# A decoder layer on one core: first keys turned by channel halves, and the opening of group 0 put in another order

## What is computed

```
x = layernorm(x + mixer(x))          # RMS norm, in-projection, causal conv of 4 taps, SiLU,
                                     # y = (C B^T * exp(cs_i - cs_j) * causal) (dt * hid) + D * hid,
                                     # gate, group RMS norm, out-projection
x = layernorm(x + softmax(x K^T) K)  # K: 1500 keys of 512 channels for each sequence
x = layernorm(x + ffn(x))            # base product + top-2 of 8 low-rank experts
```

## Time and profile before

| | |
|---|---|
| median of 3 runs | 1479.44 us (1477.43 to 1480.03) |
| the profiled execution's own time | 1479.15 us |
| its span | 1477.4 us |
| PE busy | 1420.3 us, 96% of the span |
| DVE, ACT, POOL busy | 67%, 51%, 34% |
| granted TensorE clock, mean | 0.99 |
| DMA | 142.60 MB, mean 97 GB/s |

### The profile page before, as it was taken

One profiled execution on the slowest core, in us unless ns is written; L12 is line 12 of the kernel. 1 busy time (PEld: TensorE's weight loads), 2 busy tenths in 40 slices (PEclk: granted clock), 3 DMA queues, 4 the chain that ended last, 5 costly groups with the idle time before them and its releaser, 6 DMA issues.

```text
span 1477.4 us, 30164 instructions
## 1 busy us (share of the span) xinstructions
PE 1420.3 (96%) x12816; PEld 1169.2 (79%) x12816; DVE 993.2 (67%) x1313; ACT 752.2 (51%) x1003; POOL 496.0 (34%) x368
## 2 busy tenths in 40 slices
PE   5899999999999999999999999999999978999995
PEld 4798989898989888888888888889888864445442
DVE  5784768476847684767476757765775676888764
ACT  5765636463756274636463656365536443543340
POOL 5253435242524253425342434333433320111101
PEclk9999999999999999999999999999999999999998
DMA  4431213121312131213221312221221365566610
GB/s 150 118 106 54 82 51 99 47 90 47 98 58 88 40 98 58 81 45 100 65 74 53 97 55 73 58 91 55 73 65 55 131 240 195 217 242 261 195 44 13
DMA packets 53347, 142.60 MB, mean 97 GB/s; under 512 B 9777, under 2 KB 9905, under 8 KB 46951
## 3 DMA queue, kind: packets, MB, share of 16 engines
q1 hardware_dynamic: 51518, 137.01, 28.3%
q0 software_dynamic: 1696, 3.67, 0.8%
HBM read 136.53 MB, written 2.29 MB: 94 GB/s over the span
## 4 chain that ended last, share of the span: by engine, by line
PE 83%; DVE 7%; issue 4%; DMA 3%; ACT 1%; POOL 1%; SPq 0%; DVEq 0%; POOLq 0%; ACTq 0%
PE bank L1174 47%; PE bank L1242 20%; PE bank L1217 5%; PE bank L1204 4%; DVE keysT L934 3%; DMA x1p<-acc 2%; PE bank L1477 2%; PE bank L1392 2%; PE bank L1448 1%; DMA ring_a<-in_context 1%; PE bank L1274 1%; DVE conv L809 1%; PE bank L1229 1%; PE bank L1444 0%; DVE part L770 0%
## 5 line engine op out<-in xcount | busy, mean ns | idle before, releaser
L1174 PE MATMUL bank<-h_hi,w_hi 128*128 128x448 f32 x1152 | 338.2, 375 | 2.2 <-DVE conv L809 2.2
L432 POOL TENSOR_TENSOR y_lo<-yg,y_hi 128x896 fp32r<-128x896 f32 x63 | 134.2, 2129 | 578.6 <-ACT y_hi L605 538.5
L1174 PE MATMUL bank<-h_lo,w_hi 128*128 128x448 f32 x1152 | 328.0, 366 | 0.0
L1174 PE MATMUL bank<-h_hi,w_lo 128*128 128x448 f32 x1152 | 327.1, 365 | 0.0
L809 DVE SCALAR_TENSOR_TENSOR conv<-bank,conv_w,conv 128x880 f32<-128x880 f32 (+2 forms) x240 | 268.0, 1117 | 85.6 <-ACT conv L578 79.8
L1174 PEld LDWEIGHTS bank<-h_hi,w_lo 128*128 128x128 f32 x1152 | 216.8, 188 | 17.4
L1174 PEld LDWEIGHTS bank<-h_lo,w_hi 128*128 128x128 f32 x1152 | 216.9, 188 | 17.2
L416 POOL TENSOR_TENSOR w_lo<-w_raw,w_hi 128x512 fp32r<-128x512 f32 x144 | 188.3, 1308 | 119.1 <-ACT w_hi L544 117.6
L1174 PEld LDWEIGHTS bank<-h_hi,w_hi 128*128 128x128 f32 x1152 | 208.2, 188 | 20.1 <-DVE conv L809 2.6
L854 DVE TENSOR_TENSOR hd_dt<-bank,dt_j 128x512 f32<-128x512 f32 x128 | 82.4, 685 | 208.0 <-PE bank L1204 208.0
L1242 PE MATMUL bank<-wo_hi,y_hi 128*128 128x512 f32 x420 | 165.2, 393 | 0.0
(11 more groups left out here) (181 smaller groups left out, 1932.1 us busy)
## 6 DMA issues: line engine op xcount, KB each, us to landing
w_raw<-in_w_in SPq DMA_DIRECT2D x144, 256.0 KB, 2.8
decay<-cs_scratch SPq DMA_DIRECT2D x128, 196.0 KB
ring_a<-in_context SPq DMA_DIRECT2D x24, 1024.0 KB, 7.9
ring_b<-in_context SPq DMA_DIRECT2D x21, 1024.0 KB
wo_raw<-in_w_out SPq DMA_DIRECT2D x64, 256.0 KB, 2.6
ring_b<-in_context SPq DMA_DIRECT2D x3, 896.0 KB
acc<-in_x SPq DMA_DIRECT2D x1, 1792.0 KB, 8.5
out<-z POOLq DMA_DIRECT2D x16, 112.0 KB, 2.7
```

The source lines that it names most:

```text
L432: g_.tensor_tensor(y_lo[:, c % 4, :], yg[:, c % 2, :], y_hi[:, c % 4, :].bitcast(f32), ALU.subtract).then_inc(s["y_low"], 1)
L1174: last = mm(place, w[:, k * P:(k + 1) * P], x[:, k, half * HALF:(half + 1) * HALF], start=(k == 0 and i == 0), stop=(k == KT - 1 and i == 2))
```

## The change

It touches two places, the opening with group 0, and the handover.

- `x` comes in three pieces (2, 2 and 3 tiles). The transposes of `x`, and the splits behind them, run over all channel blocks of tiles 0 to 3 first, then over all of tiles 4 to 6. POOL waits with its first split of a weight until all tiles are scaled. Several memsets and the two small operations at L940 and L941 stand first in DVE's queue.
- The conv taps of B and C stand ahead of the running sum on DVE. The copy to `cs_all` goes from DVE to ACT. The token-major transposes go behind `cb_product` (three of four) and `project(0, 4)` (the fourth), into four other banks. `mask_cb` of group 0 goes ahead of the differences, and the first five differences, distances and exponentials are spread over steps 0 to 2. The loads of weights 6 and 7 go ahead of the store of `cs_all`.
- At the handover, `keys_part(0, 0, 0)` goes ahead of the last two `add_skip`, and the order of the parts becomes: half 0 of unit 0, half 1 of unit 0, half 0 of units 1 and 2, half 1 of units 1 and 2. `score_first` makes each channel block over all keys at once, in the order 0, 4, 1, 5, 2, 6, 3, 7, then 8 to 15. `turn_first_queries` goes ahead of the last part of the out-projection. All remaining `last_sum`, and the statistics of tiles 1 to 3, are made before the loop over pairs, and the tiles' norms run one earlier all through the loop.

```diff
-            sp.dma_start(part[:, 0:4, :], x[:, 0:4, :]).then_inc(x_loaded[0], 16)
-            sp.dma_start(part[:, 4:TT, :], x[:, 4:TT, :]).then_inc(x_loaded[1], 16)
+            for i, (lo, hi) in enumerate(((0, 2), (2, 4), (4, TT))):
+                sp.dma_start(part[:, lo:hi, :], x[:, lo:hi, :]).then_inc(x_loaded[i], 16)
...
-            for idx in range(2, 6):
+            for idx in range(2, 8):
                 load_w(0, idx)
 
-            sp.wait_ge(s["dt_dve"], 6)
+            sp.wait_ge(s["cs_all_set"], 1)
...
+            pool.wait_ge(s["h_scaled"], TT)
             pool.wait_ge(s["dtw_hi"], 1)
...
             ln1_scale(1)
+            load_x1(1)
             ln1_scale(2)
-            load_x1(1)
+            ln1_scale(3)
...
                         first_tap(g, 2 + 2 * st, g * CT + st, 2 + st)
                         if first and st == 0:
-                            dt_token_major()
+                            act.wait_ge(s["dt_dve"], 5)
+                            a(real(cs_all), seqs(sq[:]), ACT.Copy).then_inc(s["cs_all_set"], 1)
+                        if first and st == 1:
+                            dt_token_major(3)
+                            exps(0, 0, 1)
...
                         if first and st == 0:
-                            for c in range(3):
-                                distance(0, c)
+                            for i in range(3):
+                                dt_token_major(i)
+                            distance(0, 0)
+                        if first and st == 1:
+                            distance(0, 1)
+                            distance(0, 2)
+                            exps(0, 1, 3)
+                        if first and st == 2:
+                            distance(0, 3)
+                            distance(0, 4)
+                            exps(0, 3, 4)
...
-            dve.wait_ge(s["dt_dve"], 4)
-            v.tensor_tensor_scan(sq[:], keep, yg[:, 0, :], 0.0, ALU.mult, ALU.add).then_inc(s["dt_dve"], 1)
-            dve.wait_ge(s["dt_dve"], 5)
-            v.tensor_copy(real(cs_all), seqs(sq[:])).then_inc(s["dt_dve"], 1)
+
+            def running_sum():
+                dve.wait_ge(s["dt_dve"], 4)
+                v.tensor_tensor_scan(sq[:], keep, yg[:, 0, :], 0.0, ALU.mult, ALU.add).then_inc(s["dt_dve"], 1)
...
                         taps(g, 1, g + GROUPS * CT + GROUPS, 1)
+                        if first:
+                            running_sum()
                     scale_hid(g, st - 1)
                     taps(g, 2 + 2 * st, g * CT + st, 2 + st)
                     wo_low(g, st - 2)
                     if first and st == 0:
-                        dve.wait_ge(s["cst_evac"], 4)
-                        for c in range(3):
-                            differences(0, c)
-                    differences(g, st + 3)
+                        mask_cb(0)
+                        dve.wait_ge(s["cst_evac"], 2)
+                        differences(0, 0)
+                    elif first and st == 1:
+                        weigh(0, 0)
+                        differences(0, 1)
+                        differences(0, 2)
...
+            keys_part(0, 0, 0)
             add_skip(LAST, CT - 2)
...
             wo_low(LAST, CT - 2)
-            keys_part(0, 0, 0)
+            keys_part(0, 0, 1)
...
-            keys_part(0, 0, 1)
+            keys_part(0, 1, 0)
             group_squares(GROUPS)
...
-            for half in range(2):
-                keys_part(0, 1, half)
+            keys_part(0, 2, 0)
+            keys_part(0, 1, 1)
+            keys_part(0, 2, 1)
             for t in range(4, TT):
                 last_halves(t)
-            for half in range(2):
-                keys_part(0, 2, half)
-            for t in range(1, 3):
+            for t in range(1, TT):
                 last_sum(t)
-                norm1_stats(t)
+                if t < 4:
+                    norm1_stats(t)
...
-                if u == 0:
-                    for t in range(3, TT):
-                        last_sum(t)
...
+            turn_first_queries()
             last_part(6, 7).then_inc(s["outb_done"], 1)
-            turn_first_queries()
...
-                for c in range(4):
-                    if c < 3:
-                        pe.wait_ge(s["q0_part"], c + 1)
-                    else:
+                for b in (0, 4, 1, 5, 2, 6, 3, 7):
+                    if b < 3:
+                        pe.wait_ge(s["q0_part"], b + 1)
+                    elif b == 3:
                         pe.wait_ge(s["q_set"], 1)
-                    if c == 0:
+                    if b == 0:
                         pe.wait_ge(s["kT_set"], 8)
-                    for k in range(KT):
-                        score_block(4 * k + c, 0, 2 * KB)
+                    last = score_block(b)
+                last.then_inc(s["s_mm"], 1)
                 pe.wait_ge(s["kT_set"], 12)
-                for b in range(NB):
-                    last = score_block(b, 2 * KB, KJ)
-                    if b % 8 == 7:
-                        last.then_inc(s["s_mm"], 1)
+                for b in range(8, NB):
+                    last = score_block(b)
+                last.then_inc(s["s_mm"], 1)
```

More of the change, by code:

```diff
@@ L530, in _ @@
             for t in range(TT):
[L531 removed]
+                act.wait_ge(x_loaded[min(t // 2, 2)], 16)
                 if t:
@@ L643, in group @@
                 for st in range(steps):
-                    if not (first and st == 0):
+                    if not (first and st < 3):
                         distance(g, st + 2)
-                    exp_step = live and st % 4 == 1
+                    exp_step = live and st % 4 == 1 and not (first and st == 1)
                     if exp_step:
@@ L740, in _ @@
             queries(0, range(4))
-            first_norm(1)
-            first_norm(2)
+            for t in range(1, 4):
+                first_norm(t)
             for u in range(PAIRS):
@@ L763, in _ @@
             v = nc.vector
+            v.memset(hid[:].rearrange("p a n -> p (a n)"), 0.0)
+            keep = sqsum[:]
+            v.memset(keep, 1.0).then_inc(s["dt_dve"], 1)
+            dve.wait_ge(s["dt_dve"], 1)
+            v.memset(keep.rearrange("p (b i) -> p b i", i=LEN)[:, :, 0:1], 0.0)
+            dve.wait_ge(s["zeroed"], 1)
+            v.tensor_reduce(own[:], ident[:].rearrange("p (i a) -> p a i", a=SUB), AX.X, ALU.add)
+            v.tensor_copy(causal[PAD:P, :], causal_hi[PAD:P, :]).then_inc(s["dstep"], 1)
+            dve.wait_ge(s["dstep"], 1)
             for i, (lo, hi) in enumerate(((0, 4), (4, TT))):
@@ L771, in _ @@
                                     ALU.mult).then_inc(s["h_scaled"], 1)
-            v.memset(hid[:].rearrange("p a n -> p (a n)"), 0.0)
-            for k in range(KT):
-                for r, n in ((0, 4), (1, 3)):
+            for r, n in ((0, 4), (1, 3)):
+                for k in range(KT):
                     i = 2 * k + r
-                    dve.wait_ge(s["h_evac_hi"], i + 1)
+                    dve.wait_ge(s["h_evac_hi"], KT * r + k + 1)
                     v.scalar_tensor_tensor(out=h_lo[:, k, r * 512:r * 512 + n * P],
@@ L958, in group @@
                     multiply_gate(g, st - 2)
-                    weigh(g, st - 1)
+                    if not (first and st == 1):
+                        weigh(g, st - 1)
                     if st == 0:
@@ L974, in group @@
                             add_output(g, t)
-                    if st == 0:
+                    if st == 0 and not first:
                         mask_cb(g)
             over_groups(dve, group)
+            keys_part(0, 0, 0)
             add_skip(LAST, CT - 2)
@@ L1349, in group @@
                         cb_product(g)
+                        if g == 0:
+                            for i in range(3):
+                                dt_token_major(i)
                     if g == LAST and st == CT - 1:
@@ L1375, in _ @@
             last_ready(6)
-            for t in range(6):
+            for t in range(5):
                 last_part(t, 6)
             sum_last_squares()
+            last_part(5, 6)
             last_ready(7)
```

87 lines of the change are left out of this document (43 added, 44 removed).

## The result

| | before | after |
|---|---|---|
| median, runs side by side | 1478.43 us (1475.14 to 1480.03) | 1464.77 us (1461.32 to 1465.61) |
| ratio to before | | 0.9899 (0.9887 to 0.9912) |
| span of the profiled execution | 1477.4 us | 1463.9 us |
| PE busy | 1420.3 us | 1416.2 us |
| granted clock, mean | 0.99 | 0.992 |

In the profiles PE is the engine of the matmuls, PEld its weight loads, DVE, ACT and POOL are those of the other operations, and SP issues most of the DMAs. A product's 24 matmuls stand as x24 in the chain of waits.

What follows compares the result with a forecast made beforehand. PE was taken as busy nearly the whole span, with idle time to gain only in the opening and the handover. Terms 4.7 + 5.5 + 6.4 = 16.6 us off 1479.15 gave 1462.5, range 1455 to 1471.

Steps and rivals of the forecast that it cites:

- a clock of 0.50 in group 0: Sign of being wrong: PE's granted clock at half speed anywhere in group 0.
- The front, 5.0: Opening up to the `dt` product: earlier squares, faster scaling and `hid` memset off the chain start it 5.0 us earlier.
- Up to step 0, 9.9 earlier: Opening from the `dt` product to step 0: `project(0, 4)` starts 9.9 us earlier, 5.0 of `project(0, 2)`'s 10.1 from before.
- What is late next: Rest of group 0: late decay tiles and taps leave gaps in steps 1 to 3, so 4.7 of 9.9 us is gained.
- That the opening gives everything back, at 0.14: Rival: the opening's gain is given back; chance 0.14.
- The first scores, 5.5: Handover, first pair's scores: earlier start and half the instructions end them at 1212.1, a gain of 5.5 us, bounds 2 and 7.3.
- The 1.8 left for a short gap: Within the first scores: 1.8 us allowed for one short gap or a stretch at clock 0.50.
- Behind the first scores, 0: Between the first scores and the second pair's scores: no change counted, 0 us.
- The second pair, 6.4: Second pair: keys requested sooner, stretch from scores to probabilities takes 6.0 instead of 12.4 us, gaining 6.4, bounds 0 and 6.6.
- The slower case, a late unit 0: Rival: first keys' transposes wait for unit 0 and delay the last y product; 1482.5 at 20 us lateness, chance 0.04.
- That the handover keeps its waits: Rival: gaps in `score_first` and waits for `x1p` stay, handover gains 4 instead of 11.9 us: 1470.4, chance 0.10.
- DVE and ACT did not keep up: Rival that they keep up in steps 1 to 3: gaps close, opening worth 9.9 us, 1457.3; chance 0.10.

Runs made afterwards that it cites:

- the kernel with one early tap: Changed kernel with ACT's first conv tap of hidden channels and split of weight 10 made earlier in step 3 of group 0; 1462.81 us, ratio 0.989.
- the opening alone: Kernel before with only the opening and group 0 as changed, its handover as before; 1476.98 us, ratio 0.9987.
- The kernel with twice the instructions: Changed kernel with each first-score block made in two sets of matmuls, over 8 and 4 key columns; 1472.66 us, ratio 0.9949.
- late sums: Changed kernel with `last_sum` of tiles 4 to 6 back between the first and second pair on DVE; 1469.21 us, ratio 0.9927.
- The kernel with both early taps: Changed kernel with ACT's first tap and weight split made earlier in steps 3 and 4 of group 0; 1461.47 us, ratio 0.9876.
- the handover alone: Kernel before with only the handover as changed, its opening as before; 1466.72 us, ratio 0.9918.

## Why the prediction was right, and where it was off

1462.5 was forecast and 1464.77 came, a gain of 16.6 against 13.7. The mechanisms were those of the forecast; of its terms one was too small, two were too large, and one was missing. One of the signs that it had named for being wrong came, a clock of 0.50 in group 0, and one came in part: PE waited 4.15 us for `x1p`, for the second pair's queries, though not behind that pair's scores.

- **The front, 5.0: right.** `dt` product at 17.75 for 17.8. The scaling of three tiles takes 1.28; the forecast had 1.25. POOL's splits now start at 14.00, when it is over; in the kernel before they ran from 13.88 to 17.95, beside the 4.28. That the splits stretched it is the reading; no run moves them alone. The running sum took 2.67 us from 37.38 on, with a split beside it from 36.86 to 38.16, and 3.00 before, with two from 34.91 to 39.27.
- **Up to step 0, 9.9 earlier: right.** `project(0, 2)` at 33.55 for 33.7, at clock 1.00. `project(0, 4)` starts at 45.84 for 56.32, 10.5 earlier, as only 12 of the 16 transposes, 1.46 for 2.0, lie ahead of it. The 1.85 for the fall of the clock holds for the profile it was read from: of the three executions of the old opening one had no fall.
- **What is late next: the gaps were right, their price was not.** Forecast gaps of 1.6, 0.5 and 3.1 in steps 1 to 3; measured 1.23 behind `mixw` in step 1, almost none in step 2 and 3.21 in step 3 (the whole stretch from 60 to 88 has 3.36 of idle PE). But the gap of 3.21 brought the clock down, and the product behind it took 6.72 instead of 4.86: 1.86. The sum took the gaps alone and had no term for the fall of the clock. Out of 4.7 came 3.75, and the kernel with one early tap, where gap and fall are gone, starts the out-projection 2.7 earlier. That the opening gives everything back, at 0.14, was so half right: the clock fell behind one gap only, and by this profile 3.75 were left. By the times of whole runs it gave back more: the opening alone is worth 1.6 us in the medians. The profile of the kernel before, from which the 3.75 are counted, is the least lucky of three: they start the first out-projection at 116.00, 114.63 and 114.36, and five of the new opening at 111.88 to 112.25. Against the other two the new opening is ahead by 2.1 to 2.8, not 3.75.
- **The first scores, 5.5: too small.** 7.1 came, near the upper bound of 7.3. The 1.8 left for a short gap was not used: there is none. The kernel with twice the instructions shows that the step from half the instructions to no gap was right. The condition it was given, that loads fill the DMA engines, is not needed for a gap: one of 1.67 comes without load.
- **Behind the first scores, 0: missing, -3.3.** The prediction carried the gain of the scores through the first pair's softmax and values as if that stretch stayed as it was. It grew from 15.9 to 19.2. Before, PE turned the second pair's queries as soon as the scores ended, the `x1p` rows being there, and reached the transposes of the probabilities after 3.51. Now scores end 10.9 earlier, but the copy to `x1p` is issued only 6.9 earlier (1201.92 for 1208.85), and it holds PE until 1210.84, when the probabilities are ready too (the three copies in question take 6.1 to 7.8 us to land, 4.0 to 5.3 in the kernel before, where they are issued later). So the turn of the queries comes behind the wait: 5.05 to the transposes, 1.5 more. And PE, idle 4.15 in one piece, has its clock at 0.50 behind it: transposes 1.2 more, values 0.6 (in the second profile, where the low clock is shorter, the values take 10.45, less than before). The copies are slow because of the keys' loads: with units 3 to 5 held back they land in 1.9 to 3.4 us, and with the feed-forward weights out of the way (late sums) still in 6.0 to 7.5. The kernel with both early taps shows the clock's part: with matmuls in the wait the fall and 2.0 us go.
- **The second pair, 6.4: slightly large.** 5.3 came: the stretch behind the scores is 5.8 for 6.0, but the scores themselves take 11.8 instead of 10.5, with a gap of 0.45. What the other 0.9 is stays open; in the second profile they take 10.5, and a wait of 1.54 for `x1p` stands behind them. The cause was right: late sums alone bring back 4.4 us and the wait of 11.65.
- **Rivals.** The slower case, a late unit 0, had no sign in the rows: no transposing of keys stood in the way of the last y product. That the handover keeps its waits was half right (the DMA engines' share was 1.00 to 1.03 from 1198 to 1210 in the kernel before): the gaps in the first scores went, but PE waits as long for `x1p` in all as before, 7.5 us, and the longest of these waits, 4.15, now stands behind the first scores. DVE and ACT did not keep up.

The terms add up: 3.75 + 7.1 - 3.3 + 5.3 = 12.85, and 0.7 from the later pairs make the 13.5 of the span. That the handover alone is worth 11.8 in the medians, where 5.5 + 6.4 = 11.9 was forecast, is partly luck: a term too small by 1.6 stands against one missing and one too large by 1.1.

## What to carry to other kernels

When a stall is moved, carry the lateness through the next stages on every engine and price the gap that is left with what the clock does behind it: here 3.21 us of idle PE cost another 1.86. When a stage is shortened, look at what it used to cover: the first scores, 7 us shorter, laid bare a small copy that they had covered until then. And before an effect of under 2 us is read from a profile, look at a second execution of the same kernel. Two things may be worth a try. Where PE waited 4.63 us for the small copies, 20 matmuls that nothing needs, 4.73 us long, brought the median down by 2.0 us. And the first scores in 256 matmuls instead of 128 wider ones, with the same products, cost 7.9 us, with 6.4 of gaps.

## What the runs showed of the hardware that was not expected

- The place at which the granted clock falls is not fixed by the program: the same opening had it under a product at 45 us in one execution, under transposes at 40 us in another and not at all in a third; the first out-projection starts at 116.00, 114.63 and 114.36. Behind the first scores idle stretches of 4.15 and 4.63 us were followed by 0.50, one of 3.83 (the late sums) by 0.50 as well, and one of 3.85 by 1.00. How long it stays low varies too: 6 us and 3 us in two executions of the changed kernel.
- Score matmuls of 116 to 256 columns stall at places 128 records apart: 0.98 and 3.61 us under loads, 0.21 and 1.67 with nearly idle DMA engines, 1.04, 3.29 and 2.03 in the split version. With up to 384 columns for each the first pair shows no such gap, the second one of 0.45.
- Three copies of 32 to 112 KB from one SBUF tile to another land in 6.1 to 7.8 us while the keys' loads run, and in 1.9 to 3.4 us with these held back.
- A table load of ACT ahead of a SiLU does not always run while ACT waits for the SiLU's input. In the kernel before, one at 39.03 ran at once and the activation behind it waited 3.42. Here one stands idle 3.01 with the activation and then adds its 1.28 behind the last conv tap. Why it is so at one place and not at the other stays open.

```profile
71.65 1.28 ACT L587 ACT_TABLE_LOAD   x1 [3.01 <-DVE conv L829]
```
